# Fused mLSTM layer: overlapped ghost blocks, masks from ScalarE, three raw weight buffers, 65-column value products

## The reference, cut to what matters

```python
def _mlstm_parallel(q, k, v, i_pre, f_pre):      # 8 heads, dqk 32, dv 64
    logfg = jax.nn.log_sigmoid(f_pre)
    Fcum = jnp.cumsum(logfg, axis=-1)
    Dmat = Fcum[..., :, None] - Fcum[..., None, :] + i_pre[..., None, :]   # causal
    m = jnp.max(Dmat, axis=-1, keepdims=True)
    C = einsum(q, k) / sqrt(dqk) * exp(Dmat - m)
    n = jnp.maximum(jnp.abs(jnp.sum(C, axis=-1, keepdims=True)), jnp.exp(-m))
    h = jnp.einsum('bhst,bhtd->bhsd', C / n, v)
# block: h_in = rmsnorm(x); q, k, v, o from it; x1 = x + (sigmoid(o) * norm(h)) @ w_out
#        h2 = rmsnorm(x1); x1 + (silu(h2 @ w_gate) * (h2 @ w_up)) @ w_down
# ghost: w = lut[idx];  (silu(x @ gate.T) * (x @ up.T)) @ down.T
xn = _layernorm(x)
x = x + _L0_attn_ref(xn, ...) + _L0_ffn_ref(xn, ...)
```

## Time and profile before

| | |
|---|---|
| median of 3 runs | 2892.45 us (2889.81 to 2893.76) |
| the profiled execution | 2881.09 us |
| its span, first to last instruction | 2879.3 us |
| TensorE busy | 2558.6 us, 89% |
| VectorE, ScalarE, GpSimd busy | 48%, 29%, 22% |
| mean granted TensorE clock | 0.949 of full |
| DMA | 508.94 MB, mean 177 GB/s |

### The profile page before, as it was taken

One profiled execution on the slowest core, in us unless ns is written; L12 is line 12 of the kernel. 1 busy time (PEld: TensorE's weight loads), 2 busy tenths in 40 slices (PEclk: granted clock), 3 DMA queues, 4 the chain that ended last, 5 costly groups with the idle time before them and its releaser, 6 DMA issues.

```text
span 2879.3 us, 33321 instructions
## 1 busy us (share of the span) xinstructions
PE 2558.6 (89%) x11152; PEld 2045.8 (71%) x11152; DVE 1382.3 (48%) x2444; ACT 837.6 (29%) x1522; POOL 628.6 (22%) x496
## 2 busy tenths in 40 slices
PE   6667999899899999889989988999889889889888
PEld 5345787687677777768767766777767767767767
DVE  4543645674675675567367466611323313323323
ACT  4323214434433442443443344211111111111111
POOL 2533221221221222132122122211111111111111
PEclk9578999999999999999999999999999999999999
DMA  4555442354255346136435424654654664664664
GB/s 147 209 201 215 147 168 92 132 192 158 96 182 218 103 154 241 63 124 217 155 120 187 177 106 154 234 201 167 249 212 160 245 223 165 245 221 165 248 217 164
DMA packets 121659, 508.94 MB, mean 177 GB/s; under 512 B 11376, under 2 KB 11376, under 8 KB 88080
## 3 DMA queue, kind: packets, MB, share of 16 engines
q1 hardware_dynamic: 115152, 494.89, 48.4%
q10 hardware_dynamic: 6336, 11.80, 1.2%
HBM read 434.69 MB, written 71.96 MB: 176 GB/s over the span
## 4 chain that ended last, share of the span: by engine, by line
PE 44%; issue 38%; POOL 7%; DVE 6%; DMA 2%; ACT 2%; DVEq 0%; POOLq 0%; SPq 0%; ACTq 0%
PE acc L561 10%; PE up_bank L561 9%; PE gate_bank L561 8%; PE bank_b L561 5%; PE bank_a L561 5%; POOL hidden_lo L1648 4%; PE bank_a L637 2%; PE bank_b L634 1%; PE bank_a L596 1%; DMA gu<-mlp_parts 1%; DVE look_w L1244 1%; PE bank_b L644 1%; PE bank_b L626 1%; DMA raw_dn<-w_dn 1%; POOL vw L1679 1%
## 5 line engine op out<-in xcount | busy, mean ns | idle before, releaser
L561 PE MATMUL gate_bank<-act_hi,gu 128*128 128x512 f32 x1728 | 605.4, 412 | 99.5 <-DMA gu<-ghost_parts 71.7
L1648 POOL TENSOR_TENSOR hidden_lo<-hm,hidden_hi 128x512 fp32r<-128x512 f32 x216 | 285.0, 1319 | 1480.2 <-ACT hidden_hi L860 1480.2
L561 PE MATMUL up_bank<-act_hi,gu 128*128 128x512 f32 x1728 | 593.9, 405 | 0.0
L561 PE MATMUL acc<-dn,hidden_hi 128*128 128x512 f32 x1728 | 559.7, 406 | 32.5 <-POOL hidden_lo L1648 32.5
L561 PEld LDWEIGHTS gate_bank<-act_hi,gu 128*128 128x128 f32 x1728 | 341.1, 197 | 184.5 <-issue 105.5
L1249 DVE SCALAR_TENSOR_TENSOR th<-th,gate_bank 128x512 f32<-128x512 f32 x216 | 147.6, 683 | 579.5 <-ACT th L855 579.5
L561 PEld LDWEIGHTS acc<-dn,hidden_hi 128*128 128x128 f32 x1728 | 326.6, 195 | 100.6 <-POOL hidden_lo L1648 20.3
L561 PEld LDWEIGHTS up_bank<-act_hi,gu 128*128 128x128 f32 x1728 | 326.7, 189 | 80.9 <-issue 13.5
L561 PE MATMUL gate_bank<-act_lo,gu 128*128 128x512 f32 x864 | 350.8, 406 | 0.0
L561 PE MATMUL acc<-dn,hidden_lo 128*128 128x512 f32 x864 | 344.2, 398 | 0.0
L561 PE MATMUL up_bank<-act_lo,gu 128*128 128x512 f32 x864 | 338.6, 392 | 0.0
(11 more groups left out here) (213 smaller groups left out, 3204.0 us busy)
## 6 DMA issues: line engine op xcount, KB each, us to landing
gu<-mlp_parts SPq DMA_DIRECT2D x128, 1024.0 KB, 5.2
gu<-ghost_parts SPq DMA_DIRECT2D x89, 1024.0 KB, 5.1
dn<-mlp_parts SPq DMA_DIRECT2D x128, 512.0 KB, 4.8
dn<-ghost_parts SPq DMA_DIRECT2D x88, 512.0 KB, 3.9
ghost_parts<-look_w SPq DMA_DIRECT2D x33, 512.0 KB, 3.0
mlp_parts<-gu SPq DMA_DIRECT2D x16, 1024.0 KB, 4.9
xn<-x SPq DMA_DIRECT2D x15, 1024.0 KB, 7.8
vo_w_hi<-vo_parts SPq DMA_DIRECT2D x12, 1024.0 KB, 9.7
```

The source lines that it names most:

```text
L561: mm = pe.matmul(dst, l[a], r[c], start=first and k == 0 and n == 0, stop=last and k == len(lhs) - 1 and n == 2)
L1648: pool.tensor_tensor(HH[1][:], hm[:], HH[0][:].bitcast(f32), ALU.subtract).then_inc(of.low.sem, 1)
```

## The change

It has five parts.

1. **Look-ups.** ScalarE makes three masks per chunk from the indices, by way of two helper arrays (`y`, `z`, `m1`, `m2`, `m3`); VectorE keeps bit 0 and the seven predicated copies. A plan (`plan`) is worked out when the program is built and places both engines' steps tile by tile. The loop now does 10 chunks per pass, 5 in each half (two of the 30 are padding), and `TAIL` does the last 5.
2. **VectorE's order in a unit.** The look-up steps of tiles 0 to 7 stand between `unit_2` and the norm, and the norm of odd tiles stands ahead of `unit_3`.
3. **Ghost blocks.** SyncE stores each block's transposed normalized x (`xt_parts`, 2 MB) in the stage that makes it, and reloads it for its ghost block; layer norm and transposes are gone there. The blocks are written out without a loop, the last `down` of a block stands behind the first `up` of the next, and the transfers of 1 MB stand in tiles 1 to 6, one each.
4. **First block.** MLP weights come as one 768 KB piece per tile, into two raw buffers on `act1`'s place and a third on `raw_gu` for the last four tiles; splitting starts in the first front, and four tiles are left for the second. The second block's layer norm comes early (`x_raw`), the output projection of the first block goes to the `ACC` banks, and its second norm's transposes stand in the next front.
5. **Value products.** They move 65 columns instead of 128.

Outside the core of the diff, `store_vo` moves from the start to `SECOND`'s tile 2, the final result is stored in four pieces, and semaphores are renamed.

```diff
-STEPS_V, STEPS_A = 10, 9
-LEVELS = [0, 1, 3, 2, 5, 7, 6, 4]
-TAKEN = [[4] * 8 + [4, 0, 0, 5, 5, 4, 0, 0], [5] * 8 + [4, 0, 0, 5, 6, 5, 0, 0]]
+STEPS_V = 7
+STEPS_A = ["y", 3, "z", 2, "m1", 4, 5, "m3", 0, 1, 7, "m2", 6, "upper"]
+ROOM_V = [[0, 0] + [2] * 6 + [3, 3] + [4] * 5 + [0]] * 2 + [[3] * 15 + [0]]
+ROOM_A = [[5] * 8 + [7] * 7 + [0]] * 2 + [[7] * 15 + [0]]
...
-                    mm = pe.matmul(A[:, h * P:(h + 1) * P], ct[:, h, :], va[:, c:c + P], start=True, stop=True)
+                    mm = pe.matmul(A[:, h * P:h * P + VS], ct[:, h, :], va[:, c:c + VS], start=True, stop=True)
...
+            def store_xt(n, parts):
+                for s in range(2):
+                    src = parts[s][:, :, :].rearrange("p k n -> p (k n)").bitcast(f32)
...
+                    sp.dma_start(dst, src).then_inc(st_xt, 16)
+            def load_xt(n, s):
+                dst = XH[n % 2][s][:, :, :].rearrange("p k n -> p (k n)").bitcast(f32)
+                sp.dma_start(dst, xt_parts[n, s]).then_inc(ld_xt[n % 2], 16)
...
+                if what == "y":
...
+                    ins = act.activation(yz[:, 0, :], ix[:, n % 2, :], ACT.Abs, bias=-7.5)
+                elif what == "z":
+                    act.wait_ge(look_act, in_act(at, n, "y"))
+                    ins = act.activation(yz[:, 1, :], yz[:, 0, :], ACT.Abs, bias=-4.0)
+                elif what == "m1":
+                    act.wait_ge(look_act, in_act(at, n, "z"))
+                    ins = act.activation(mask_of(n, 1), yz[:, 1, :], ACT.Relu, bias=-2.0)
...
             for t in range(NM):
...
+                        unit_2(t)
+                        if looks(at):
+                            look_up(at, steps_taken(half, t))
+                        if t % 2:
+                            norm_1(t // 2)
+                        unit_3(t)
...
+            behind = (MLP, (BATCH, -1), NM - 1)
+            for n in range(BATCH * HALVES):
+                at = (BATCH + n // HALVES, n % HALVES)
+                for t in range(NF):
+                    gate(GHO, at, t, XH[at[1]])
+                    up(GHO, at, t, XH[at[1]])
+                    of, place, k = behind
+                    down(of, place, k, NM - 1 if of is MLP else NF - 1)
+                    behind = (GHO, at, t)
+            down(GHO, at, NF - 1, NF - 1)
...
+                    if t in (1, 2) and n + 1 < len(blocks):
...
+                        load_xt(n + 1, t - 1)
...
+                        sp.dma_start(rest[half], rows_of(x, n * TOK)).then_inc(ld_rest[0], 16)
...
+                    for m in range(3):
+                        mlp_lo_(m)
                     mx_(0)
+                    mlp_lo_(3)
```

More of the change, by code:

```diff
@@ L60, with steps_taken, uppers_by @@
+PLANS = [plan(kind) for kind in range(3)]
+def steps_taken(kind, t):
+    return PLANS[kind][t][0]
+def uppers_by(kind, t):
+    return span_of(kind)[1] if t == NM - 1 else PLANS[kind][t][2]
 CAP = 15.0
@@ L475, in tiles @@
                 mb = previous(at)
-                stored = 0
+                kind = look_kind(at)
+                stored = span_of(kind)[0]
+                if not here(at, TAIL):
+                    wait(sp, vec_xT, mb, NB - 1, "lo")
+                    sp.sem_inc(sp_passed, 1)
+                    store_xt(b * HALVES + half, XH[half])
                 for t in range(NM):
@@ L551, in _ @@
+            last = blocks[-1]
+            for i in range(NB):
+                first = (BATCH * HALVES - 1) * TOK + i * P
+                wait(sp, vec_out, last, i)
+                sp.dma_start(out[first:first + P, :], rest[last[1]][:, i, :]).then_inc(st_out[last[1]], 16)
+            sp.wait_ge(st_out[0], 16 * (BATCH + 1))
+            sp.wait_ge(st_out[1], 16 * (BATCH + NB))
         @block.tensor
@@ L732, in front @@
                 q_k_T(at, 0)
+                if here(at, SECOND):
+                    for i in range(NB):
+                        h2_T(FIRST, i)
                 proj(at, 2)
@@ L995, in front @@
                 qkT_(0)
+                if here(at, SECOND):
+                    for i in range(NB):
+                        h2_T(i)
                 wait(act, vec_rows, at, 0, "biased")
@@ L1069, in tiles @@
                 for t in range(NM):
-                    if first and t > 10:
+                    if first and t > 8:
                         break
@@ L1467, in tiles @@
                 for t in range(NM):
+                    if first and t > 8:
+                        break
                     if stage:
@@ L1533, in tiles, with add_ghosts @@
                 for i in range(NB):
                     dve.tensor_copy(XN[half][:, i, :], ACC[i][:]).then_inc(vec_out.sem, 1)
+                if here(at, SECOND):
+                    dve.wait_ge(st_vo, 64)
+            def add_ghosts(at):
+                half = at[1] % 2
+                wait(dve, GHO.down, at, NF - 1)
+                wait(dve, vec_rest, at, 2 * NB - 1)
+                for i in range(NB):
+                    dve.tensor_tensor(rest[half][:, i, :], rest[half][:, i, :], ACC[i][:], ALU.add).then_inc(vec_out.sem, 1)
@@ new lines, in _ @@
+            for n in range(BATCH * HALVES):
+                at = (BATCH + n // HALVES, n % HALVES)
+                half = at[1]
+                for t in range(NF):
+                    gated(GHO, at, t)
+                    product(GHO, at, t)
+                    if t == 0 and n == 0:
+                        wait(dve, MLP.down, (BATCH, -1), NM - 1)
+                        for i in range(NB):
+                            dve.tensor_copy(XN[0][:, i, :], ACC[i][:]).then_inc(vec_out.sem, 1)
+                    elif t == 0:
+                        add_ghosts(previous(at))
+                    if t in (8, 9):
+                        if t == 8:
+                            for z in range(3):
+                                dve.wait_ge(ld_rest[z], 16 * (n + 1))
+                        for i in range(NB):
+                            if t == 9:
+                                wait(dve, vec_rest, at, i)
+                            dve.tensor_tensor(rest[half][:, i, :], rest[half][:, i, :], rest[t - 6][:, i, :], ALU.add)\
+                                .then_inc(vec_rest.sem, 1)
```

853 lines of the change are left out of this document (451 added, 402 removed).

## The result

The changed kernel takes **2609.74 us** (median of 4 runs, 2609.44 to 2610.12) against 2893.11 us before (4 runs, 2889.81 to 2899.07): a ratio of 0.9019, 95% interval 0.9003 to 0.9034. Forecast were 2620 us and a range of 2575 to 2695.

The account below looks back on a forecast made before the run. TensorE was taken as the bound, lengthened by waits and the half clock behind them. Savings 142.3 + 6.8 + 95 + 23 + 7 - 3 = 271 from 2881.1 gave 2610, stated as 2620 us for run-to-run offset; range 2575 to 2695.

Parts of the forecast that it names:

- Ghost blocks (142.3 + 6.8): Last 88 tiles: 728.9 us instead of 871.18, saving 142.3; step from the last MLP tile 14.95 to 8.16, saving 6.8.
- Both covers: Ghost blocks: late down product has its hidden rows ready; 1 MB reads spread over tiles 1 to 6 need 321 GB/s.
- The loop (95): Six loop halves: fewer VectorE look-up steps cut TensorE's waits for weighted scores; 43 of 137.9 us kept, 95 saved.
- 0.3 to 1 us on three odd tiles: Loop halves: norm and copies ahead of the state update delay the next scores by this much on odd tiles.
- the 0.4 on even tiles: Loop halves: five ScalarE steps behind the transposed heads make the next exponents late by about 0.4 us.
- First block (23): First block and second front: front begins 21 us earlier, second front takes 59 instead of 61.56; saving 23, bounds 5 and 35.
- Value products (7): Attention units: moving 65 instead of 128 columns saves 0.11 us per unit, 7 us over 64 units.
- Stores and index load (-3): Second block's added stores and the last MLP's gated(0) behind an index load: a charge of 3 us, at most 10.
- Ghost edges half open: Rival, 13%: transfers queue at ghost block edges, each block loses 7 us to weight loads and half clock; 2676 us.
- ScalarE as the limit: Rival, 13%: in the loop, 14 ScalarE steps per chunk instead of 9 cost another 14 us per half; 2704 us.
- Slower by the clock: Rival, 2%: without idle time TensorE's clock is held at 1.2 GHz in long dense stretches; 2975 us at half of ghost tiles.
- Everything closes: Rival, 8%: moving columns count (18 us more) and tiles 9 to 11 cost nothing (20); 2580 us.

Follow-up runs that it names:

- down_early: Changed kernel with the last down product of a ghost block ahead of the next block's gate again, transfers still spread; 2631.28 us.
- bunch: Changed kernel with the late down product kept, but the ghost blocks' transfers of tiles 3 to 6 put into tile 2; 2678.57 us.

## Why the prediction was right, and where it was wrong

**Ghost blocks (142.3 + 6.8): right, by its own steps.** 728.9 us were forecast from first gate to end, 728.72 measured; all gates stand 8.16 apart over the edges, no gate waits for ghost weights. Both covers that I named were tried: without the one or the other the stage is 17.3 or 67.4 us longer. I had allowed 40 us for lost cover of the reads, 5 per block; with five transfers in one tile it is 8.4 per block.

**The loop (95): mechanism right, size too small; 120.7 measured.** Two parts of it. "The second block, without look-ups, takes 92.51 us" was my floor, and it was none: that block lost 0.6 us from gate to gate in each of three even tiles, from the norm ahead of the next exponents, and the new order took it away (90.74), here and in all six halves. I had counted the norm's move only as a cost, to `kv`. And "0.3 to 1 us on three odd tiles" is 1.0 on one of them, the one with a bit cut; the 0.4 on even tiles didn't come, and 1.3 to 1.6 us ahead of gate(9) came that I had not. Above the floor of 90.74 this part is 2.4 us per half instead of 3.6. The floor is 11 of the 26 us missed, the smaller costs are the other 15. In tiles 9 to 11 the price was 2.2 us per half instead of 3.5: down(10) stops for 0.96 us, released by `hidden_lo` as forecast (1.4 in the sum), and the second norm makes gate(11) 1.0 us late (1.7 in the forecast).

**First block (23): wrong, -4.9 measured.** Failed is "split 1.6, lower 3.6, load about 4, some 10 us each from about 14 on, then the last store and the first load, in all 59". The first split came 18 us into the front, the period was 13.3 to 14.6 because a load behind a 1.5 MB store takes 7.6 us to its split, and the end took 11.9; in all 77.94 us. Also "3 us remain" from the last x1 to the front were 5.6. The last x1 itself was 6.5 us late: the first unit by 3.2, which I put down to the four splits of the first front that I had set at nothing "against earlier norms" (not shown apart), and by 2 to 5 through the norm's place, where I had counted a gain. The run with splits and transfers placed otherwise has its first gate at 232.17. The lower bound of 5 us for this term was too high as well.

**Value products (7): wrong, under 1.** "I take 7, since that row moves fewer columns still and is hardly cheaper": the narrow transposes have 87.5 ns each, the value products 101 ns at 65 and at 128 columns. The two kinds differ in more than their width (the rows give 16*128 for the one and 128*128 for the other), and the difference was not for me to interpolate. The Trainium skill ("TensorE: Matmul & The Clock Gate", LDWEIGHTS) gives a weight load of 128 columns 107 ns by its formula, in which the moving columns don't appear; by that rule the change saves nothing here, and it doesn't. As a price of one product the rows are below it, 101 and 87.5 ns.

**Stores and index load (-3): wrong in sign, not seen apart.** The first two tiles of the last MLP together are 1.4 us longer than before; the second block is 2.8 us shorter in spite of its stores (1.8 of it from the order), and the rest 4.2.

**The rivals.** Ghost edges half open: no, no such wait. ScalarE as the limit: a level takes 0.80 us, a mask 0.62 (below) whether it reads floats or indices, so nearly what I assumed for the mean of 0.73, and only tile 10 is late. Slower by the clock: the clock is 1.00 over 728.72 us in which TensorE is busy for 721.23. "Everything closes" (2580) needed 18 us from the columns, which cost nothing; the measured 2610 has a first block that was worse and a loop that was better than the sum.

Misses of 28 and 7 us on one side and 26 and 10 on the other cancelled. That the total came out to 1 us is luck; alone it would have seemed to confirm every term.

## What to carry to other kernels

Take the floor of a stage from counted work, not from the stage that happens to have no stalls in the list: 92.51 us looked like one, and held three losses of 0.6 us. Where an engine gets steps that wait for another engine, place them a tile behind what they wait for; copies placed in the tile of their level cost 4 to 6 us per half (with another plan for ScalarE in the run that mended it), and copies crowded into the last tile cost 6 to 8, through the one buffer behind them. Read a total of waits stage by stage before you give it to one stage. A chain of raw load, split, remainder and store on one buffer is priced as a whole, with what stands ahead of each transfer on its queue.

## What the runs showed of the hardware

- A 768 KB load asked for 0.36 us behind a 1.5 MB store on SyncE's queue had a median of 7.9 us to its landing (three loads), and 5.5 when asked for ahead of it; the store then took 8.9 instead of 6.0. The Trainium skill ("DMA: Bandwidth & Descriptors", Queues, rings and completion order) says that each DMA engine takes a queue's descriptors in order; both figures go the way it says.
- A ScalarE step over 128x512 with a scale and a bias per partition (a level) takes 803 ns, one with constants (a mask) 619. The tile view of the changed kernel (ns min/median/max):

```profile
L1044 ACT ACTIVATE look_w<-look_w,lt,ld x280: 797/803/817, 482.5 to 1835.7; 128x512 f32<-128x512 int32 x140
L1034 ACT ACTIVATE look_w<-raw_gu x35: 613/619/621, 484.4 to 1826.8; 128x512 f32<-128x512 f32 x35
```

- A stop of 2.21 us of TensorE at the ghost edges left the granted clock at 1.00 over the whole stage (`down_early`); one of 5.76 us was followed by a stretch at 0.88 (`bunch`), and eight such waits (45.8 us) made TensorE's busy time in the stage 21 us longer for the same 3181 instructions.
